# GNN layer on one core: the first normalisation rearranged, its root taken on GpSimd

## The reference

```python
xn = _layernorm(x, axis=-1)                 # (x - mean) / sqrt(var + 1e-5)
x = x + gnn(xn, edges, edge types) + mix(xn)
x2 = _layernorm(x, axis=-1)
x = x + ffn(x2)                             # one of 8 experts, chosen by the moments of x2
# gnn: q, k, v = xn @ wq.T + bq, ...; a second linear on each; 16 heads of 64;
#      scores / 8 + mask, softmax, times v2, output projection
# mask: 384 x 384, -inf where there is no edge; softplus(edge weight of the edge's type) where
#      there is one; the last of several equal edges counts; the diagonal is always set
```

## Time and profile before

| what | value |
|---|---|
| median of 3 runs | 472.8 us (472.56 to 473.14) |
| the profiled execution | 472.28 us, span 470.5 us |
| TensorE products | 462.7 us busy, 98% |
| VectorE | 341.7 us, 73% |
| ScalarE | 258.7 us, 55% |
| GpSimd | 153.4 us, 33% |
| granted TensorE clock, mean | 0.998 of full |
| chain that ended last | TensorE 91%, DMA 2%, VectorE 2%, ScalarE 2% |

### The profile page before, as it was taken

How to read it: one execution, slowest core, us unless ns; L and a number is a source line. 1 busy time by engine, 2 the same in 40 slices (tenths; PEclk the granted TensorE clock), 3 DMA queues, 4 the chain that set the end, 5 groups by cost and what they waited for, 6 DMA issues and landing times.

```text
span 470.5 us, 7320 instructions
## 1 busy us (share of the span) xinstructions
PE 462.7 (98%) x2521; PEld 429.9 (91%) x2521; DVE 341.7 (73%) x787; ACT 258.7 (55%) x423; POOL 153.4 (33%) x178
## 2 busy tenths in 40 slices
PE   7999999999999999999999999999999999999996
PEld 5999999999999888999999999999998888888885
DVE  6979876776636347688888888897875993586394
ACT  3724533333314244878979698897965362153270
POOL 4246667767777761001010202202044000050200
PEclk9999999999999999999999999999999999999999
DMA  8877776566544465477676747767669854210553
GB/s 247 324 235 213 233 213 168 180 181 184 155 131 159 129 206 197 156 236 262 198 226 205 240 154 228 246 211 232 195 210 364 276 214 135 89 45 1 169 236 134
DMA packets 39097, 91.92 MB, mean 195 GB/s; under 512 B 7458, under 2 KB 20354, under 8 KB 38932
## 3 DMA queue, kind: packets, MB, share of 16 engines
q1 hardware_dynamic: 33540, 83.02, 55.9%
q0 software_dynamic: 4864, 7.45, 4.7%
q10 hardware_dynamic: 656, 0.98, 0.6%
HBM read 77.96 MB, written 13.47 MB: 194 GB/s over the span
## 4 chain that ended last, share of the span: by engine, by line
PE 91%; DMA 2%; DVE 2%; ACT 2%; SPq 1%; issue 0%; DVEq 0%; ACTq 0%
PE PS L1327 34%; PE PS L1337 28%; PE PS L1332 17%; PE PS L1465 4%; PE PS L1453 2%; PE PS L1589 2%; PE PS L1395 2%; DMA U<-x 1%; PE PS L1315 1%; ACT U L684 1%; PE PS L1593 1%; DVE U L1303 1%; PE PS L1573 1%; DMA turn<-U 1%; DMA U<-turn 1%; ACT w_hi L561 0%
## 5 line engine op out<-in xcount | busy, mean ns | idle before, releaser
L936 DVE TENSOR_TENSOR w_lo<-raw,w_hi 128x1024 fp32r<-128x1024 f32 x86 | 104.3, 1225 | 45.8 <-ACT w_hi L561 45.7
L561 ACT ACTIVATE w_hi<-raw 128x1024 fp32r<-128x1024 f32 x87 | 91.0, 1054 | 72.8 <-PE PS L1337 46.0
L477 POOL DMA_INDIRECT table<-evalue,where x96 | 102.5, 1068 | 42.5 <-issue 26.0
L1332 PE MATMUL PS<-xT_hi,w_lo 128*128 128x384 f32 x320 | 61.9, 334 | 0.0
L1327 PE MATMUL PS<-xT_lo,w_hi 128*128 128x384 f32 x320 | 61.9, 334 | 0.0
L1327 PE MATMUL PS<-xT_hi,w_hi 128*128 128x384 f32 x320 | 61.9, 334 | 0.0
L1332 PEld LDWEIGHTS PS<-xT_hi,w_lo 128*128 128x128 f32 x320 | 56.0, 188 | 0.0
L1327 PEld LDWEIGHTS PS<-xT_lo,w_hi 128*128 128x128 f32 x320 | 56.0, 188 | 0.0
L1327 PEld LDWEIGHTS PS<-xT_hi,w_hi 128*128 128x128 f32 x320 | 56.0, 188 | 0.0
L1337 PE MATMUL PS<-w_hi,T_hi 128*128 128x512 f32 x144 | 40.1, 391 | 0.0
L1337 PE MATMUL PS<-w_hi,T_lo 128*128 128x512 f32 x144 | 39.9, 389 | 0.0
(11 more groups left out here) (247 smaller groups left out, 805.4 us busy)
## 6 DMA issues: line engine op xcount, KB each, us to landing
raw<-weights SPq DMA_DIRECT2D x84, 512.0 KB, 4.6
turn<-U SPq DMA_DIRECT2D x16, 576.0 KB, 3.8
U<-turn SPq DMA_DIRECT2D x64, 144.0 KB, 2.9
U<-key_dram SPq DMA_DIRECT2D x32, 192.0 KB, 4.2
mask<-weights SPq DMA_DIRECT2D x9, 512.0 KB, 5.1
table<-Q POOLq DMA_DIRECT2D x4, 576.0 KB
V<-conv SPq DMA_DIRECT2D x4, 512.0 KB, 5.1
U<-table POOLq DMA_DIRECT2D x3, 576.0 KB, 6.6
```

The lines of the kernel that those rows point to most:

```text
L477: pool.indirect_dma_start(tables[g], bass.IndirectOffsetOnAxis(ap=where[:, k:k + 1], axis=0), evalue[:, k:k + 1], None, bounds_check=N * N ...
L561: act.activation(w_hi[slot][:], raw[slot][:], ACT.Copy).then_inc(hi_ready[slot], 1)
L936: dve.tensor_tensor(w_lo[slot][:], raw[slot][:], w_hi[slot][:].bitcast(F32), ALU.subtract).then_inc(lo_ready[slot], 1)
L1332: last = pe.matmul(o, wl, src[0][:, k, :], start=False, stop=(k == KB - 1))
```

## The change

- Tile 0 of x is loaded in four quarters, two on each queue; tiles 1 and 2 in halves as before. SP issues the first weight tile when the second half of tile 0 has landed, and everything after it without a further wait for x; the second weight tile comes after constants and edges.
- The identity is made on GpSimd (memset and affine select). Bias columns, edge weights and expert statistics become columns of the one array of constants, loaded in one DMA.
- Statistics are joined per tile. GpSimd raises variance plus eps to the power -0.5 for each tile and computes the shift for tiles 0 and 1. ScalarE scales tiles 0 and 1, VectorE tile 2. ScalarE's table for Sqrt is not loaded at the start; that for Exp is.
- `WARM` is 17, `FILL` is gone. Jobs 0 and 1 run in another order and all over 384 columns.
- GpSimd, once VectorE has scaled tile 2, rounds half of the first weight tile and computes its low part, then makes the edge keys, stores them, and only then fills the tables.
- `row_norm` of the second normalisation no longer computes the unused shift.

```diff
-            for t in range(NT):
+            for c in range(2):
+                q = slice(c * HALF, c * HALF + HALF // 2)
+                sp.dma_start(x_rows[:, 0, q], x[0:P, q]).then_inc(x_in[0][c], 16)
+            for t in range(1, NT):
                 sp.dma_start(x_rows[:, t, 0:HALF], x[t * P:(t + 1) * P, 0:HALF]).then_inc(x_in[t][0], 16)
-            sp.wait_ge(x_in[1][0], 16)
+            sp.wait_ge(x_in[0][1], 32)
             load_weights(*A_USES[0], weights[0])
-            sp.wait_ge(x_in[2][0], 16)
-            load_weights(*A_USES[1], weights[1])
-            sp.dma_start(cst[:, C_TRI:C_ALL], consts[:, C_TRI:C_ALL]).then_inc(cst_in, 16)
+            sp.dma_start(cst[:], consts).then_inc(cst_in, 16)
             sp.dma_start(erow_i, edge_rows).then_inc(edges_in, 16)
             sp.dma_start(ecol_i, edge_cols).then_inc(edges_in, 16)
-            sp.dma_start(bias[:], bias_cols).then_inc(const_in, 16)
-            sp.dma_start(disc_in[:], disc).then_inc(const_in, 16)
+            load_weights(*A_USES[1], weights[1])
             load_weights(*A_USES[2], weights[2])
...
-            pool.dma_start(ew[:], edge_weights.partition_broadcast(P)).then_inc(ew_in, 16)
+            pool.memset(ident[:], 0.0).then_inc(ident_ready, 1)
...
+            pool.wait_ge(ident_ready, 3)
+            def first_root(t):
+
+                pool.wait_ge(spread_ready, 2 * t + 2)
+                pool.tensor_tensor(rstd[:, 2, t:t + 1], rstd[:, 0, t:t + 1], power[:], ALU.pow).then_inc(root_ready, 1)
+
+            for t in range(2):
+                first_root(t)
+                pool.wait_ge(root_ready, t + 1)
+                pool.tensor_scalar(rstd[:, 3, t:t + 1], mv[:, t, 0:1], -1.0, rstd[:, 2, t:t + 1],
+                                   ALU.mult, ALU.mult).then_inc(shift_ready, 1)
+            first_root(2)
+
+            slot = A_USES[0][0]
+            pool.wait_ge(xn_ready, 1)
+            pool.wait_ge(w_in[slot], 16)
+            pool.wait_ge(w_used[slot], 1)
+            pool.tensor_copy(w_hi[slot][:, 0:HALF], raw[slot][:, 0:HALF]).then_inc(first_hi, 1)
+            pool.wait_ge(first_hi, 1)
+            split_lo(*A_USES[0])
+
+            pool.wait_ge(edges_in, 32)
+            pool.tensor_copy(erow, erow_i).then_inc(key_calc, 1)
...
+            pool.dma_start(key_dram, erow[:, 0:P]).then_inc(key_out, 16)
+
             pool.wait_ge(blanked, 2)
-            pool.wait_ge(w_in[A_USES[0][0]], 16)
             for g in QUARTERS:
...
+            for t in range(2):
+                act.wait_ge(shift_ready, t + 1)
+                act.activation(xn_rows[:, t, :], x_rows[:, t, :], ACT.Identity, scale=rstd[:, 2, t:t + 1],
+                               bias=rstd[:, 3, t:t + 1]).then_inc(xn_first, 1)
+            act.wait_ge(xt_turned, 1)
+            banks, r = turned(0)
+            act.activation(xT[0][:, :, r], banks, ACT.Copy).then_inc(xt_hi, 1)
...
+            act.activation(w_hi[slot][:, HALF:D], raw[slot][:, HALF:D], ACT.Copy).then_inc(hi_ready[slot], 1)
...
+            act.activation(xT[0][:, 0:4, r], banks[:, 0:4, :], ACT.Copy).then_inc(xt_front, 1)
+            act.wait_ge(xt_turned, 4)
+            act.activation(xT[0][:, 4:KB, r], banks[:, 4:KB, :], ACT.Copy).then_inc(xt_rest, 1)
             split_hi(*A_USES[1])
+            split_hi(*A_USES[2])
...
+            dve.wait_ge(root_ready, 3)
+            dve.tensor_scalar(xn_rows[:, 2, :], x_rows[:, 2, :], mv[:, 2, 0:1], rstd[:, 2, 2:3],
+                              ALU.subtract, ALU.mult).then_inc(xn_ready, 1)
...
+            dve.wait_ge(xt_turned, 2)
+            mid, r1 = turned(1)
+            dve.tensor_copy(xT[0][:, :, r1], mid).then_inc(xt_mid, 1)
...
             turn(0, xt_turned)
-            for n in range(FILL):
-                pe.matmul(PS[:, 0, :], w_lo[2][:, 0:P], w_lo[2][:, P:P + HALF], start=True, stop=True)
+            pe.wait_ge(xn_first, 2)
+            turn(1, xt_turned)
             pe.wait_ge(xn_ready, 1)
-            turn(1, xt_turned)
-            pe.wait_ge(xn_ready, 2)
             turn(2, xt_turned, halves=True)
...
+            part_of(0, w_hi, 0, range(4), start=True)
             pe.wait_ge(hi_ready[A_SLOTS[0]], 1)
...
             pe.wait_ge(xt_rest, 1)
-            first_part(slice(P, N), range(4, KB))
+            part_of(0, w_hi, 0, range(4, KB))
+            pe.wait_ge(lo_ready[A_SLOTS[0]], 2)
+            part_of(0, w_lo, 0, range(KB))
             pe.wait_ge(hi_ready[A_SLOTS[1]], 1)
-            whole_part(1, w_hi, 0, True, False)
+            part_of(1, w_hi, 0, range(KB), start=True)
             pe.wait_ge(xt_done, NT)
-            whole_part(0, w_hi, 1, False, False)
-            pe.wait_ge(lo_ready[A_SLOTS[0]], 2)
-            whole_part(0, w_lo, 0, False, True).then_inc(w_used[A_SLOTS[0]], 1)
-            whole_part(1, w_hi, 1, False, False)
+            part_of(0, w_hi, 1, range(KB), stop=True).then_inc(w_used[A_SLOTS[0]], 1)
+            part_of(1, w_hi, 1, range(KB))
             pe.wait_ge(lo_ready[A_SLOTS[1]], 2)
-            whole_part(1, w_lo, 0, False, True).then_inc(w_used[A_SLOTS[1]], 1)
+            part_of(1, w_lo, 0, range(KB), stop=True).then_inc(w_used[A_SLOTS[1]], 1)
```

More of the change, by code:

```diff
@@ L47 @@
 SLOTS = 3
-WARM = 21
-FILL = 4
+WARM = 17
 FIRST = 32
@@ L106, with gps_layer @@
 LN_BANKS = ((6, 4, 2), (6, 4, 0))
-C_ID, C_TRI, C_ONES, C_EIDX, C_ONE, C_ALL = 0, 128, 256, 384, 392, 520
-def gps_layer(nc, x, out, weights, conv, down, upT, up_b, down_b, conv_b, disc, bias_cols,
-              rows, edge_weights, edge_rows, edge_cols, consts):
+C_TRI, C_ONES, C_EIDX, C_ONE, C_BIAS, C_EW, C_DISC = 0, 128, 256, 264, 392, 464, 468
+C_ALL = C_DISC + 2 * EXPERTS * KB
+def gps_layer(nc, x, out, weights, conv, down, upT, up_b, down_b, conv_b, rows, edge_rows, edge_cols, consts):
     with ExitStack() as ctx:
@@ L161, in gps_layer @@
         cst = sb("cst", [P, C_ALL], F32)
-        ident = cst[:, C_ID:C_ID + P]
+        ident = sb("ident", [P, P], F32)
+        power = sb("power", [P, 1], F32)
         tri = cst[:, C_TRI:C_TRI + P]
@@ L595, in _ @@
-            act.activation(rstd[:, 1, 1:NT], rstd[:, 0, 1:NT], ACT.Sqrt).then_inc(rstd_guess, 1)
-            for t in range(NT):
-                act.wait_ge(xt_turned, t + 1)
-                banks, r = turned(t)
-                ks = slice(0, 4 if t == 2 else KB)
-                act.activation(xT[0][:, ks, r], banks[:, ks, :], ACT.Copy).then_inc(xt_hi, 1)
-                if t == 0:
-                    split_hi(*A_USES[0])
+            act.activation(tiny[:, 24:25], w_lo[2][:, 0:1].bitcast(F32), ACT.Exp)
@@ new lines, in _ @@
+            for t in range(2):
[5 more added lines that the diff above has]
+            act.activation(xT[0][:, :, r], banks, ACT.Copy).then_inc(xt_hi, 1)
+            slot = A_USES[0][0]
+            act.wait_ge(w_in[slot], 16)
+            act.wait_ge(w_used[slot], 1)
@@ L608, in _ @@
             act.activation(ew_t[:, 0:4], ew_t[:, 0:4], ACT.Ln, bias=1.0).then_inc(aprep, 1)
-            act.wait_ge(const_in, 32)
-            for a in range(2, DEPTH):
-                split_hi(*A_USES[a])
+            act.wait_ge(cst_in, 16)
             for a in range(FIRST):
@@ L870, in row_stats, with row_norm @@
                 dve.tensor_scalar(rstd[:, 0, t:t + 1], mv[:, t, 1:2], EPS, None, ALU.add).then_inc(var_ready, 1)
-            def row_norm(which, t, done):
-                v, y, z, m = (rstd[:, c, t:t + 1] for c in range(4))
-                dve.wait_ge(rstd_guess, t + 3)
+            def row_norm(t, done):
+                v, y, z = (rstd[:, c, t:t + 1] for c in range(3))
+                dve.wait_ge(rstd_guess, t + 1)
                 step(dve.reciprocal(y, y))
@@ L880, in row_norm @@
                 step(dve.tensor_tensor(z, z, y, ALU.mult))
-                dve.scalar_tensor_tensor(out=m, in0=mv[:, t, 0:1], scalar=-1.0, in1=z,
-                                         op0=ALU.mult, op1=ALU.mult).then_inc(rstd_ready, 1)
-                if which or t != 1:
-                    dve.tensor_scalar(xn_rows[:, t, :], x_rows[:, t, :], mv[:, t, 0:1], z,
-                                      ALU.subtract, ALU.mult).then_inc(done, 1)
+                dve.tensor_scalar(xn_rows[:, t, :], x_rows[:, t, :], mv[:, t, 0:1], z,
+                                  ALU.subtract, ALU.mult).then_inc(done, 1)
             def turned(t, which=0):
@@ L895, in first_stats @@
                 for c in range(2):
[L896 removed]
+                    dve.wait_ge(x_in[t][c], 16 if t else 32)
                     half_stats(t, c)
[L899 removed]
+            for t in range(NT):
+                first_stats(t)
                 dve.wait_ge(norm_step, normed[0])
[L902 to L907 removed]
@@ L909, in first_roots @@
-            def first_roots(ts, guess):
-                c = slice(ts[0], ts[-1] + 1)
-                v, y, z = (rstd[:, n, c] for n in range(3))
-                dve.wait_ge(rstd_guess, guess)
-                step(dve.reciprocal(y, y))
```

(11 more changed lines are left out.)

153 lines of the change are left out of this document (62 added, 91 removed).

## The result

The changed kernel takes 474.9 us (median of 22 runs, 471.5 to 478.4) where the one before takes 472.7 (22 runs beside it, 471.9 to 474.0). The ratio is 1.0047, 95% interval 1.003 to 1.0064: slower by 2.2 us, and with a spread that the kernel before doesn't have. Ratios, and the ranges given beside them, leave out a run that lies over 1.5% above the fastest of its kernel. The forecast was 470.6 and faster. The profiled execution took 475.0 us (span 473.1).

What follows compares the result with a forecast made beforehand. TensorE, busy 98% of the span, was taken to bound the kernel, so only job 2's start counted: profiled 472.28 us less 2.2 is 470.1, plus 0.5 for the median, 470.6; own range 469.9 to 471.4, 8 in 10 469.6 to 472.9.

Steps and rivals of the forecast that it cites:

- so it is hardly later: GpSimd's first scatter, at 30.11 us before, was to start hardly later although the table fills move behind the keys.
- 29.0 at the latest: End of the wait for the table fills: last issue by 18.5 us plus 10.5, against 24.22 before.
- Tile 1 is issued a slot later but limited by bytes: 5.6 to 5.8.: Load of x's second tile: landing set by bytes, at 5.6 to 5.8 us, despite the later issue.
- Rival 2: Tile 2 of x lands at 8.0 to 8.6 us, ScalarE's queue sharing with weights; total 471.5; chance 0.14.
- Tile 0's last quarter: Load of x's first tile in quarters: first half at 3.8 us, last at 4.3, variance at 5.5.
- The root: Power of one column on GpSimd, replacing Sqrt and four small steps: 0.4 us, hand-offs included.
- Tile 2's variance: VectorE's statistics of x's third tile: landing at 6.9 us, variance at 9.1 instead of 9.82.
- The low part: GpSimd's subtraction over 1024 columns: 2.66 us beside VectorE, ending at 13.7, with TensorE waiting 0.6.
- Job 2: TensorE's start of its third job, the measure of the change: 20.7 us instead of 22.90, 2.2 earlier.
- the software packets' hole: DMA gap from 5.0 to 5.5 us, 148 GB/s, laid to the edge-weight broadcast; the change takes the broadcast away.
- rival 3: Root on GpSimd too slow: at 2.4 us each, 1.4 us slower, 474.2; chance 0.10.
- Rival 1, the clock: TensorE's clock falls over 4.6 us of transposes alone, first real products at half pace; gain 1.2, 471.6; chance 0.16.

Runs made afterwards that it cites:

- b_fills_late: The kernel before with its four table fills issued by GpSimd behind the store of the edge keys; 477.5 us, ratio 1.0082.
- a_halves: The changed kernel with tile 0 of x loaded in two halves again, fills still late on GpSimd; 473.8 us, ratio 1.0001.
- a_fills_sp: The changed kernel with the four table fills issued by SP behind the weight tile instead of by GpSimd behind the keys; 472.5 us, ratio 0.9993.
- a_halves_fills: The changed kernel with tile 0 of x in halves and the table fills issued by SP; 471.4 us, ratio 0.997.
- a_warm8_again: The changed kernel with tile 0 in halves, fills on SP and 8 warm-up products instead of 17, repeated on another chip; 471.3 us, ratio 0.9978.
- a_short: The changed kernel with 48 of the 96 scatters left out, so the mask lacks half of its edges; 474.0 us, ratio 1.0013.
- b_quarters: The kernel before with tile 0 of x loaded in quarters, nothing else; 476.3 us, ratio 1.0061.
- a_last_quarters: The changed kernel with fills on SP, tiles 0 and 1 of x in halves and tile 2 in quarters; 470.7 us, ratio 0.9967.
- a_clock_fills: The changed kernel with fills on SP, quarters kept, 21 warm-up products and four products between transposes again; 472.4 us, ratio 0.9992.
- a_rows_fills: The changed kernel with fills on SP and tile 0 in four transfers of 64 rows with 2 KB packets; 495.8 us on a slower chip, ratio 1.002.

## Why the prediction was wrong

1. **"so it is hardly later. It would matter little: the mask is folded at 184.40 and first read at 185.67, 1.3 us of cover, and the scatters follow the keys, which follow TensorE."** This step failed, and it has the larger price. The fills ended at 30.35, not "29.0 at the latest": from the last issue to the end they took 10.0 us, 0.5 less than forecast, but the last issue was out at 20.3, not 18.5, since the keys were stored at 16.50, not 14.8. The first scatter came 1.3 later. And the scatters don't follow the keys. They follow one another, as their line shows in seven kernels (us):

| | first | last | between | waited for keys |
|---|---|---|---|---|
| before | 30.1 | 169.1 | 139.0 | 7.1 |
| after | 31.4 | 172.2 | 140.8 | 1.4 |
| b_fills_late | 34.4 | 176.2 | 141.8 | 1.6 |
| a_halves | 30.7 | 174.3 | 143.6 | 0.5 |
| a_fills_sp | 29.0 | 168.3 | 139.3 | 5.9 |
| a_halves_fills | 27.4 | 168.2 | 140.8 | 5.8 |
| a_warm8_again | 26.0 | 163.9 | 137.9 | 4.7 |

The 96 scatters take 138 to 144 us wherever they start. (On the chip with the cut clock they took 146 to 156 us, 11 to 24 us of it waiting for the keys, so there the keys did hold them back; at full clock they don't.) The kernel before shows it, in the view of the scatters' line (durations in ns, then idle time by what ended it: us, times), which the forecast didn't read:

```profile
L477 POOL DMA_INDIRECT table<-evalue,where x96: 970/974/2026, 30.1 to 169.1; - x96
...
  issue: 26.0, 76
  DMA table<-evalue,where: 9.5, 16
  DVE where L999: 7.1, 4
```

Of the 7.1 us of waiting for the keys, 5.12 stand before the first scatter; the other 2 are all that 96 scatters wait for TensorE's side. A queue that is full from end to end doesn't catch up on a late start, and its own length differs by up to 5.7 us between profiles. With the fills on SP most of that stays under the cover (a_halves_fills: 470.4 to 473.0); with the late fills it reaches the total (a_halves: 470.6 to 475.4). In the profiled run the table loads ended 5.0 later: 1.3 of start, 1.8 of scatters and 2.0 of a pause between the loads; 4.15 of it is left at the fold, against 1.3 of cover. Price in the medians: 2.4 us by a_fills_sp, 0.9 by a_short.

2. **"Tile 1 is issued a slot later but limited by bytes: 5.6 to 5.8."** Failed, 6.7 to 8.4 in five traces with tile 0 in column quarters; the rate from 3.5 us falls with small transfers first. The forecast took bytes over rate as fixed. Price in the medians: 1.1 us in the changed kernel, 3.6 in the kernel before, where the clock fell as well. Rival 2 had the right shape, a late tile, at the wrong tile and by the wrong cause: with halves and the early release of the weights tile 2's statistics begin at 7.35 to 7.64, in time.

3. **Mis-sized, not wrong.** Tile 0's last quarter was read from 4.67, not 4.3, its variance there at 5.79, not 5.5; with halves it is at 5.80, so the quarters bought nothing. The root: 0.57 for 0.4 (taken from a line through two other operations), shift 0.27 for 0.2. Tile 2's variance with halves is at 9.05 (forecast 9.1), the first product at 12.38 (11.7). The low part took 2.38 to 2.40, not 2.66, no contention with VectorE, and ended at 13.70 as forecast; so the 0.7 that the first product lost is the 0.6 of waiting that didn't come. Job 2 at 20.79, forecast 20.7. But the forecast took each microsecond at job 2 for one of the total: in the profile of a_halves_fills 2.11 us at job 2 are 1.57 at the last product, and in the medians 1.2.

4. **Right.** VectorE scales alone in 0.81; the software packets' hole at 5.0 us is gone (no such packets, and 340 GB/s there in the profile after, 148 before; in a_halves the rate is 197 all the same); jobs 0 and 1 lose nothing to cut rows; products at 334 ns; rival 3, a slow root, didn't occur. Two readings were off without effect: the mean rate to 5.0 us is 195 GB/s, not 196, and the 2.4 us that GpSimd's subtractions were said to lie far below is itself one of them, over 1024 columns.

5. **Rival 1, the clock**, was given 0.16 by the cause of few products among the transposes. That cause doesn't show. In a_last_quarters TensorE runs nothing but 24 transposes from 7.10 to 12.53 us (its timeline), and the granted clock stays at 1.00. In a_warm8_again it rises from 0.50 to 1.00 before the first product at 13.40, behind transposes alone (busy times of two stretches; third from the end is the granted clock).

```profile
8.47 1.06 PE L1316 MATMUL PS<-ident,U 128*128 128x128 f32 x8 [1.37 <-ACT U L623]
9.93 1.97 PE L1316 MATMUL PS<-ident,U 128*128 128x128 f32 x16 [0.39 <-ACT U L623]
```

```profile
12.00:12.50 0.50, 0.50 (x5) 0.50 (x4) 0.50 (x1) 0.00 (x0) 0.50 (x1) 0.59 0.93 352
12.50:13.00 0.50, 0.50 (x5) 0.32 (x3) 0.50 (x1) 0.34 (x1) 0.50 (x1) 1.00 1.02 393
```

That speaks against the rule of the Trainium skill (TensorE: Matmul & The Clock Gate, Part 4: PE-mode transpose) as the forecast weighed it here. What stands before a fall of the clock is idle time: 3.06 us (a_warm8_again), 3.18 (a_short) and 3.29 (b_quarters); after 2.93 (a_fills_sp), 1.75 (a_clock_fills) and 1.37 us (after) it held. One stretch's length doesn't settle it: in a_rows_fills it fell behind 2.28 and 1.12 us with eight transposes between them, on the chip whose clock was also cut elsewhere. The price at job 2 was 1.0 in a_warm8_again and 2.0 in a_short against a_fills_sp, 0.1 of it tile 1 landing later; the rival had half of 1.0 to 3.6. So the slow clock is real and its trigger was misread.

How much of the 2.2 us is the clock's stays open. The mean granted clock is 0.996 or below in 13 of the 22 runs of the changed kernel, which took 476.2 us in mean, against 473.3 for the other nine; in the kernel before it is so in none of 83 runs on the two chips of the experiments whose clock wasn't cut elsewhere, and in a_halves_fills and a_last_quarters in none of 22. But a low clock may only mark the runs with a late tile or a late mask: in a_warm8_again 5 of 11 runs have it and are no longer than the rest (471.1 and 471.6). Warm-up products put back into the changed kernel with its fills left late would have told; it wasn't run.

With both faults out, the rest of the change is faster, but by less than forecast: 471.4, or 470.7 with tile 2 in quarters (the two aren't told apart), against 472.7. That is 1.2 or 2.0 us of the forecast 2.2. Only these two versions and a_warm8_again beat the kernel before by their intervals.

## What to carry to other kernels

Before a step is moved behind another, follow the queue that consumes it and ask whether that queue has slack after its start: the row that tells is the one that splits its idle time by releaser. A cover that one profile shows is worth less than it reads when the work under it varies by more from run to run. Cutting the first load smaller let its reader start 0.3 to 0.4 us sooner here, brought tile 0's variance no sooner (5.79 with quarters, 5.80 with halves), and cost the next load 1 to 3: look at the second landing, not the first.
